# Layer 0 of the second pass by three products of half the columns in place of four

## The reference, cut to what matters

```python
def _layer(x, style, w, b, mw, mb, typ):
    s = style @ mw.T + mb
    weight = SCALE * w * s[:, None, :, None]
    demod = lax.rsqrt(jnp.sum(weight * weight, axis=(2, 3)) + EPS)
    weight = weight * demod[:, :, None, None]
    # 'same': convolution of width 3; 'upsample': transposed one of stride 2, then a blur;
    # 'downsample': blur, then a convolution of stride 2.  Each adds its bias.
...
x = x + _L0_attn_ref(_L0_cond_ref(x, cond, ...), ...)     # four layers, then a long convolution (S4)
x = x + _L0_ffn_ref(_L0_cond2_ref(x, cond, ...), ...)     # four layers, then a routed LoRA layer
# _L0_ffn_ref: xf @ W_base.T + b_base, plus for each row the two best of 8 experts:
#   softmax of their two logits times (xf @ A_e.T) @ B_e.T * 2
```

## Time and profile before

| | |
|---|---|
| median of 3 runs | 1373.13 us (1370.47 to 1373.22) |
| the profiled execution | 1369.01 us, its span 1367.2 us |
| granted TensorE clock, mean | 0.995 |
| PE busy | 1318.5 us (96%), 8319 matmuls |
| DVE busy | 1089.6 us (80%) |
| ACT busy | 821.6 us (60%) |
| POOL busy | 796.6 us (58%) |
| chain that ended last | PE 78%, DVE 11%, ACT 3%, POOL 3% |

### The profile page before, as it was taken

The page is one execution under the profiler, slowest core; times in us unless marked ns, Lnnn a source line. Parts: engine busy times, 40 slices in busy tenths (PEclk is TensorE's granted clock), DMA queues, the critical chain, the costliest instruction groups (busy, mean ns, idle before and its releaser), DMA issues.

```text
span 1367.2 us, 23437 instructions
## 1 busy us (share of the span) xinstructions
PE 1318.5 (96%) x8319; PEld 1245.9 (91%) x8319; DVE 1089.6 (80%) x2613; ACT 821.6 (60%) x1649; POOL 796.6 (58%) x598
## 2 busy tenths in 40 slices
PE   4799999999999999999999999999999999999998
PEld 3588898999899998899999989999999999999998
DVE  7887777777777777778888999788887878788883
ACT  4587777777778787775554444545455554554440
POOL 6367766666667667665555454545555555545542
PEclk9899999999999999999999999999999999999999
DMA  3234444444445564454262432524334252424423
GB/s 130 83 105 130 129 130 130 130 130 129 130 130 137 149 146 122 116 160 113 79 151 76 123 103 76 143 84 121 105 99 128 76 150 76 135 92 116 111 78 90
DMA packets 85990, 158.64 MB, mean 116 GB/s; under 512 B 26473, under 2 KB 47858, under 8 KB 85746
## 3 DMA queue, kind: packets, MB, share of 16 engines
q1 hardware_dynamic: 84610, 155.18, 40.9%
q10 hardware_dynamic: 1264, 1.96, 0.4%
HBM read 94.18 MB, written 33.56 MB: 93 GB/s over the span
## 4 chain that ended last, share of the span: by engine, by line
PE 78%; DVE 11%; ACT 3%; POOL 3%; issue 2%; DMA 2%; SPq 0%; DVEq 0%; POOLq 0%; ACTq 0%
PE psum L1678 25%; PE psum L1680 25%; PE psum L1679 24%; DVE psum L1469 2%; PE psum L1786 1%; DVE vm_l L1437 1%; DMA vm_f<-vv 1%; DMA m0f<-in_m_dram 1%; DVE xr L1486 1%; DVE a_f L1448 1%; DVE a_l L1443 1%; DVE xr L1490 1%; POOL vbuf L848 1%; POOL vbuf L844 1%; ACT u_h L1072 1%
## 5 line engine op out<-in xcount | busy, mean ns | idle before, releaser
L1678 PE MATMUL psum<-wt_h,u_h 128*128 128x386 f32 (+1 forms) x760 | 261.7, 344 | 0.0
L1680 PE MATMUL psum<-wt_h,u_l 128*128 128x386 f32 (+1 forms) x760 | 257.8, 339 | 0.0
L1679 PE MATMUL psum<-wt_l,u_h 128*128 128x386 f32 (+1 forms) x760 | 257.6, 339 | 0.0
L1469 DVE STREAM_TRANSPOSE psum<-vbuf 32x256 f32<-32x256 f32 x480 | 218.8, 456 | 11.8 <-ACT vbuf L1050 0.7
L844 POOL TENSOR_TENSOR vbuf<-vbuf 128x512 f32<-128x512 f32 x64 | 98.7, 1542 | 218.0 <-ACT vbuf L1064 218.0
L1443 DVE SCALAR_TENSOR_TENSOR a_l<-psum,tabs,a_h 128x512 fp32r<-128x512 f32 x128 | 95.7, 751 | 162.9 <-ACT a_h L1032 162.8
L858 POOL TENSOR_TENSOR vm_f<-vm_f 128x512 f32<-128x512 f32 x64 | 82.8, 1293 | 224.3 <-DVE vm_l L1437 224.1
L1678 PE MATMUL psum<-a_h,vm_h 128*128 128x256 f32 x512 | 150.7, 294 | 4.8 <-ACT vbuf L1057 4.7
L1057 ACT ACTIVATE vbuf<-psum,tabs 128x512 f32<-128x512 f32 x128 | 105.6, 825 | 76.4 <-PE psum L1680 74.2
L869 POOL TENSOR_TENSOR xs_l<-xin,xs_h 128x1024 fp32r<-128x1024 f32 x64 | 142.1, 2221 | 14.8 <-ACT xs_h L1018 14.8
L1431 DVE SCALAR_TENSOR_TENSOR vv<-psum,vv 128x192 f32<-128x192 f32 (+2 forms) x384 | 137.2, 357 | 13.2
(11 more groups left out here) (307 smaller groups left out, 3932.6 us busy)
## 6 DMA issues: line engine op xcount, KB each, us to landing
vm_f<-vv SPq DMA_DIRECT2D x256, 112.0 KB, 3.4
xin<-in_x_ph_dram SPq DMA_DIRECT2D x32, 512.0 KB, 4.5
xr<-in_x_row_dram SPq DMA_DIRECT2D x32, 512.0 KB, 5.1
x1d<-xr SPq DMA_DIRECT2D x64, 256.0 KB, 3.3
xin<-x1d SPq DMA_DIRECT2D x32, 512.0 KB, 5.2
xr<-x1d SPq DMA_DIRECT2D x64, 256.0 KB, 5.9
xo<-in_b_base_dram SPq DMA_DIRECT2D x32, 512.0 KB, 4.3
out_dram<-xo SPq DMA_DIRECT2D x31, 512.0 KB, 3.0
```

Of the source, the lines that this page charges most:

```text
L1469: ins = V.transpose(ps_x[to, :, :].rearrange("p b (k n) -> p b k n", n=P)[:, :, :, frm], v3[frm, :, :].rearrange("p b (k n) -> p b k n", n ...
L1678: nc.tensor.matmul(to, stat_h, mov_h, start=first_ and n == 0, stop=False, skip_group_check=True)
L1679: nc.tensor.matmul(to, stat_h, mov_l, start=False, stop=False, skip_group_check=True)
L1680: ins = nc.tensor.matmul(to, stat_l, mov_h, start=False, stop=end, skip_group_check=True)
```

## The change

For tiles from `THREE = TILES + 3` = 35 on, layer 0 is computed from three products over 256 columns of each of the two batches, so each is one bank of 512 columns. With the even and the odd columns of the input apart (`xp`), one product takes the odd columns with the sum of the two matrices (`ms`), and it is shared by the even and the odd output columns; the other two take a difference of neighbouring input columns each (`d0`, and the one that replaces the odd columns in `xin`) with one of the matrices. The shared product goes to `ps_pair`. ACT evacuates it (`odd_product`), DVE adds the two others to it (`halves`), ACT and DVE split the results (`halves_high`, `halves_low`). The column sums are additions on POOL now (`neighbours`), as are the input differences (`differences`). Buffers are reused: `d0` lies in the last part of `vbuf`, its split in the last third of `lag`, the even half and the sums in tables of the first pass.

POOL's new order in `body(i)`: `vs_l`, `combined(i)`, `neighbours(i+1)`, `differences(i+2)`, `column_sums_low(i+1)`, `xo`, `inputs(i+2)`, `pair_sums(i+1)`. ACT: `inputs(i+2)` and `halves_high(i+1)` come before `row_ends(i)`, `pads(i+1)` behind `composed1`. DVE: `halves(i+1)` before the transposes, `halves_low(i+1)` between `router_end` and `composed2`.

```diff
+THREE = TILES + 3
...
+    def three(g):
+        return here(g) and g >= THREE
...
+    d0 = vbuf[:, 2 * H:].rearrange("p (b m) -> p b m", b=2)
+    a_even = old[:, 0:H].rearrange("p (b m) -> p b m", b=2)
+    sums_of = (old[:, H:H + Q], sh.em1[:, 0, :, :].rearrange("p q n -> p (q n)"))
+    msum, ms_h, ms_l = m0f[:, 0, 0, :], m0_h[:, 0, 0, :], m0_l[:, 0, 0, :]
... POOL
+            def differences(g):
+                pool.wait_ge(in_scaled, at(g))
+                pool.wait_ge(v3_val, at(g - 2))
+                G.tensor_scalar(d0[:, :, 0:1], xin[:, :, 0:1], -1.0, None, ALU.mult)
+                G.tensor_tensor(d0[:, :, 1:Q], xin[:, :, 1:H - 1:2], xin[:, :, 2:H:2], ALU.subtract).then_inc(in_diff, 1)
+                pool.wait_ge(in_diff, since(g, 2, 0))
+                G.tensor_tensor(xin[:, :, 1:H:2], xin[:, :, 1:H:2], xin[:, :, 0:H:2], ALU.subtract).then_inc(in_diff, 1)
+            def neighbours(g):
+                pool.wait_ge(y_out, since(g, 2, 1))
+                for b in range(2):
+                    ins = G.tensor_tensor(sums_of[b], a_f[:, b, :], a_even[:, b, :], ALU.add)
+                ins.then_inc(as_sum, 1)
             def inputs(g):
                 pool.wait_ge(in_hi, at(g))
+                if three(g):
+                    G.tensor_tensor(xp_l ..., xin ..., xp_h ..., ALU.subtract)          # 1024 columns, parities apart
+                    G.tensor_tensor(d0_l ..., d0, d0_h ..., ALU.subtract).then_inc(in_lo, 1)   # 512 columns
+                    return
... POOL, body(i)
                 if here(i):
                     combined(i)
+                if three(i + 1):
+                    neighbours(i + 1)
+                if three(i + 2):
+                    differences(i + 2)
+                if three(i + 1):
+                    column_sums_low(i + 1)
...
+                    if three(i + 2):
+                        inputs(i + 2)
                     if here(i + 1):
                         pair_sums(i + 1)
+                    if here(i + 1) and not three(i + 1):
                         column_sums_low(i + 1)
... ACT
+            def odd_product(g):
+                act.wait_ge(as_lo, at(g - 1))
+                act.wait_ge(a_lo, at(g - 1, 2, 1))
+                for b in range(2):
+                    A(a_f[:, b, 0:1], ..., ACT.Identity, bias=...)
+                act.wait_ge(l0_done, at(g, 2, 1))
+                for b in range(2):
+                    ins = A(a_even[:, b, :], ps_pair[:, Q * b:Q * b + Q], ACT.Copy, scale=tab(c, t, b, T_S1))
+                ins.then_inc(shared_out, 1)
+            def halves_high(g):
+                for r, (src, o) in enumerate(((a_f[:, :, :], 1), (a_even, EVEN + 1))):
+                    act.wait_ge(y_out, since(g, 2, r))
+                    A(a_h[:, :, o:o + Q], src, ACT.Copy).then_inc(a_hi, 1)
             def pair_evacuated(g, b):
+                if three(g + 1):
+                    act.wait_ge(in_lo, at(g + 1))
... DVE
+            def halves(g):
+                ve.wait_ge(shared_out, since(g))
+                ve.wait_ge(as_lo, at(g - 1))
+                for r, (to, o) in enumerate(((a_f, 1), (a_even, 0))):
+                    if r:
+                        ve.wait_ge(y_out, since(g, 2, 0))
+                    for b in range(2):
+                        ins = V.scalar_tensor_tensor(out=to[:, b, o:Q], in0=ps_x[:, r, Q * b + o:Q * b + Q],
+                                                     scalar=tabs[:, c, T_S1, batch(t, b)], in1=a_even[:, b, o:Q],
+                                                     op0=ALU.mult, op1=ALU.add)
+                    ins.then_inc(y_out, 1)
+            def halves_low(g):
+                for r, (src, o) in enumerate(((a_f[:, :, :], 1), (a_even, EVEN + 1))):
+                    ve.wait_ge(a_hi, at(g, 2, r))
+                    V.tensor_tensor(a_l[:, :, o:o + Q], src, a_h[:, :, o:o + Q].bitcast(F32), ALU.subtract).then_inc(a_lo, 1)
... DVE, turn(g, 0, 4): waits for v3_fix and y_out of g + 1 in place of v3_fix, a_lo and as_sum
... PE
             def layer0(g):
                 pe.wait_ge(in_lo, at(g))
+                if three(g):
+                    product(ps_x[:, 0, :], [(m0_h[:, c, 0, :], m0_l[:, c, 0, :], d0_h, d0_l)], True, True)
+                    product(ps_x[:, 1, :], [(m0_h[:, c, 1, :], m0_l[:, c, 1, :], xp_h[:, H:L], xp_l[:, H:L])], True, True)\
+                        .then_inc(l0_done, 1)
+                    pe.wait_ge(pair_out, at(g - 1, 2, 1))
+                    product(ps_pair, [(ms_h, ms_l, xp_h[:, 0:H], xp_l[:, 0:H])], True, True).then_inc(l0_done, 1)
+                    return
...
+                    if three(i + 1):
+                        pe.wait_ge(shared_out, since(i + 1))
                     nc.tensor.transpose(ps_hwT, hw[:, :], ident[:, :]).then_inc(pe_hwT, 1)
```

More of the change, by code:

```diff
@@ L905, in body @@
                 else:
+                    if three(i + 2):
+                        inputs(i + 2)
                     if here(i + 1):
                         pair_sums(i + 1)
+                    if here(i + 1) and not three(i + 1):
                         column_sums_low(i + 1)
-                    if here(i + 2):
+                    if here(i + 2) and not three(i + 2):
                         inputs(i + 2)
@@ L1002, in column_sums @@
                 act.wait_ge(as_sum, at(g))
+                if three(g):
+                    for b in range(2):
+                        ins = A(as_h[:, b, 0:Q], sums_of[b], ACT.Copy)
+                    ins.then_inc(as_hi, 1)
+                    return
                 A(as_h[:, :, 0:Q], a_f[:, :, :], ACT.Copy).then_inc(as_hi, 1)
@@ L1138, in body @@
                     A(bt_h, xo[:, :], ACT.Copy, scale=LORA).then_inc(bt_hi, 1)
-                if here(i + 1):
+                if three(i + 1):
+                    odd_product(i + 1)
+                elif here(i + 1):
                     layer0(i + 1)
+                if three(i + 2):
+                    inputs(i + 2)
+                if three(i + 1):
+                    halves_high(i + 1)
                 if by_blocks(i):
@@ L1153, in body @@
                 if here(i + 2):
-                    inputs(i + 2)
+                    if not three(i + 2):
+                        inputs(i + 2)
                     inputs_high(i + 2)
+                if turn_is(i, TILES):
+                    act.wait_ge(ms_sum, 1)
+                    act.wait_ge(l0_done, at(TILES - 1, 2, 1))
+                    A(ms_h, msum, ACT.Copy).then_inc(ms_hi, 1)
                 if chunk(i):
@@ L1162, in body @@
                     composed1(i + 2)
+                if three(i + 1):
+                    pads(i + 1)
                 if turn_is(i, 2):
@@ L1451, in layer0 @@
                 ins.then_inc(as_sum, 1)
+            def halves(g):
+                c, t = place(g)
+                ve.wait_ge(shared_out, since(g))
[3 more added lines that the diff above has]
+                        ve.wait_ge(y_out, since(g, 2, 0))
+                    for b in range(2):
+                        ins = V.scalar_tensor_tensor(out=to[:, b, o:Q], in0=ps_x[:, r, Q * b + o:Q * b + Q],
[6 more added lines that the diff above has]
+                    V.tensor_tensor(a_l[:, :, o:o + Q], src, a_h[:, :, o:o + Q].bitcast(F32), ALU.subtract).then_inc(a_lo, 1)
             def turned(g):
@@ L1464, in turn @@
                     ve.wait_ge(v3_fix, at(g))
-                    ve.wait_ge(a_lo, at(g + 1, 2, 1))
-                    ve.wait_ge(as_sum, at(g + 1))
+                    if three(g + 1):
+                        ve.wait_ge(y_out, since(g + 1, 2, 1))
+                    else:
+                        ve.wait_ge(a_lo, at(g + 1, 2, 1))
+                        ve.wait_ge(as_sum, at(g + 1))
                 for n in range(n0, n1):
@@ L1639, in body @@
                     inserted(i)
-                if here(i + 1):
+                if three(i + 1):
+                    halves(i + 1)
+                elif here(i + 1):
                     layer0(i + 1)
@@ L1653, in body @@
                     router_end(place(i - 1)[1])
+                if three(i + 1):
+                    halves_low(i + 1)
                 if here(i + 1):
```

41 lines of the change are left out of this document (40 added, 1 removed).

## The result

The changed kernel takes 1574.97 us (median of 4 runs, 1573.1 to 1577.73) against 1371.8 (4 runs, 1369.88 to 1373.22): a ratio of 1.1484, 95% interval 1.1459 to 1.1509. Slower, by 203 us, and 2.5 us from the forecast of 1577.5. The profiled execution took 1574.78 us, its span 1572.8.

The account below looks back on a forecast made before the run. PE was taken as the limit by 0.45 us over a 23.29 us loop; 28 turns at 30.95 instead of 23.74 (202) plus edge turns made 204.4 on 1369.0, then 4.1 to the median: 1577.5 us, range 1455 to 1620.

Parts of the forecast that it names:

- Loop and slack: Second pass before the change: the loop over POOL, DVE and ACT takes 23.29 us, 0.45 shorter than PE's turn.
- `halves_low`: DVE between router and `composed2`: two subtractions with both inputs in SBUF add 1.22 us to the loop.
- `xo` against the router: DVE's first router subtraction, wanted at 11.45, waits for POOL's `xo` until 13.5; gates come 1.9 us late, about 15.4.
- GpSimd's inputs: POOL's two instructions, 2.20 and 1.2 us, alternate with DVE's `halves_low` from 15.65, so `vm_l` ends at 21.15.
- The clock: PE idles 4.5 us before the LoRA products, its clock falls, losing 1.7 a turn; 1.2 counts, bounds 0 and 3.0.
- The sum: 28 turns at 30.95 instead of 23.74 give 202 us; the turns before and after add 1.7 and 0.8.
- The faster one: PE stays the limit at the start of `pair(i+1, 1)`, with the loop below 23.04: 1353 us, chance 0.05.
- Only `halves_low`: DVE and POOL get by each other, so each turn loses just 0.77 us: 1395 us, chance 0.07.
- Blocked, clock up: DVE and POOL block each other but PE's clock holds, 6.0 us a turn: 1544 us, chance 0.27.
- Only `xo` blocks: POOL's `inputs` fall between DVE's steps, leaving 2.7 us a turn: 1450 us, chance 0.10.
- signs named in the prediction: Profile after: turns of 29 to 32 us, PE busy 75 to 80%, waiting for `vbuf` too, router and `halves_low` stretched to 1 to 3 us.
- partly blocked case: DVE is held up by POOL's `xo` but not by its `inputs`: 1450 us, chance 0.10.

Follow-up runs that it names:

- second experiment: The changed kernel with GpSimd's `inputs(i+2)` moved behind `pair_sums(i+1)` and `column_sums_low(i+1)` moved behind those inputs: 1428.38 us, ratio 1.0422.
- filler experiment: The changed kernel with 26 unread matmuls of 256 columns put where PE waits for the LoRA operand: 1544.89 us, ratio 1.1272.
- the added pair on DVE: The kernel before with two unread 128x512 subtractions on DVE between `router_end` and `composed2`, tiles 34 to 62: 1396.36 us, ratio 1.0188.

## Why the prediction was right, point by point

**Loop and slack.** 23.29 with 0.45 of slack behind PE was the base of everything. Measured at 23.36 and 23.37.

**`halves_low`.** Priced at 1.22, measured at 1.21 (1006.88 to 1008.09).

**`xo` against the router.** It was to let the first router instruction through at T + 13.5; it ended at T + 13.25 (1005.09). The transpose of the gates was forecast at T + 15.4 and came at 15.18.

**GpSimd's inputs.** Right in sum, wrong in the instruction. The prediction has GpSimd start at T + 15.65, between the two `halves_low`, and alternate with them. In the trace GpSimd starts at T + 15.89, because ACT's split takes 1.99 and not 1.06; both `halves_low` pass at 0.69, overlapped by GpSimd only at the end of the second, and it is the two `vm_l` that are blocked, 4.80 for 1.29. The block in the sum was 2.20 + 1.2 = 3.4 and is 3.51 in the trace: GpSimd's two instructions cost 2.6 and 1.3 undisturbed (2.69 and 1.31 in the second experiment), more than the contiguous 2.20 of the earlier trace rows since they read strided. So `vm_l` ends at T + 21.05 (predicted 21.15), the LoRA operand at 22.03 (22.1), the last transpose at 24.90 (25.0). Late start and longer blocks cancelled against the earlier router; that the end came out within 0.1 is partly luck.

**The clock.** This was the unsure term, taken from one row of before, and it repeats every turn: all 28 turns have a granted clock of 0.89 to 0.95, and 27 of them a wait for `s_h` of 4.42 to 4.45 (one has 3.52). After 4.44 us without a product three matmuls of 256 columns take 0.64 (1016.13 to 1016.77 in the trace of TensorE above), and later in the turn 0.36 (1019.71 to 1020.07). The lower of the two rates, 1.2 GHz, begins in this turn a little behind the wait, at 1014.55, and lasts to 1017.84; then it is 2.4 again. Window and granted clock:

```profile
1014.55:1017.84 3.29, 3.29 (x14) 0.50 0.00 0
991.84:1022.60 30.76, 25.05 (x148) 0.94 0.28 81
```

From the LoRA products to the next T it takes 8.68 where it was 7.07, a loss of 1.61 (predicted 1.7). TensorE's own path, 22.08 + 8.68 = 30.76, closes the turn; the loop would have released it 1.1 earlier (24.90 + 1.82 = 26.72 against 27.87). The prediction took 1.2, and the filler experiment takes 1.0 of it back. What the Trainium skill says in TensorE: Matmul & The Clock Gate, section HAM oscillation — how this bites in real kernels, that waits in each tile bring the half rate back in each tile, the traces here bear out, by these numbers.

**The sum.** 28 turns (642.24 to 1514.90 after, 638.72 to 1310.82 before) are 872.66 against 672.10: 200.6 longer, forecast 202. The remaining 5.0 of the span's 205.6 lie ahead of the first such turn (3.5, of which 1.8 is already there at the start of the second pass) and behind the last (1.5); forecast 2.5. So the terms missed by 1.4 and 2.5 in opposite directions, and the difference of the medians, 203.2 against a forecast of 204.4, is closer than either by luck. The mean turn grew by 7.16, the turn shown by 7.02: two turns near 800 us are longer in both kernels, up to 27.48 before and up to 35.45 after.

**The rivals.** The faster one needed the loop under 23.04. The kernel in which PE has just the nine products, and nothing is added, shows that it isn't: 23.36, and 1359.97 us where the rival's price was 1353. "Only `halves_low`" (1395) is the added pair on DVE, 1396.36: its price was right, and it isn't this kernel. "Blocked, clock up" (1544) is what the filler gives, 1544.89. "Only `xo` blocks" (1450) is the kernel with GpSimd's inputs behind the pair sums, 1460.06: 10 us more, and its handover also waits for `d0`, which the rival did not have. These prices were worked out from rows before any of it ran.

**Signs and chances.** Two of the signs named in the prediction did not come. `halves_low` kept its 0.69 beside the start of GpSimd's work, and the subtractions that stretched are `vm_l`; PE was busy for 82%, not 75 to 80%, and did not wait for `vbuf`, since its own slow products closed the turn. And the range from 1455 on leaves out the partly blocked case at 1450 too, so by the prediction's own chances 0.28 lay outside it, not 0.18.

## What to carry to other kernels

An engine at 100% busy says that it is the limit, not how far the next one is: add up the loop between the engines for one turn before spending work on others to relieve it. Here 20 us of PE time was worth 11 at most. And price an addition on GpSimd by which VectorE instructions it will meet, not by its length: in these traces it was free beside transposes (six in 2.84, with and without) and reads of PSUM (0.87 for two), and beside a VectorE instruction with both inputs in SBUF each held the other up for a whole instruction, be it of one element (1.80 for 0.16). Moving it once more may push it onto something else (another pair of instructions, or the next DMA), so write out both queues for the whole turn.

## What the runs showed of the hardware that I had not expected

- GpSimd's memsets (five of 1024 columns in 5.00 us) leave VectorE's two-input instructions alone and stretch a `TENSOR_SCALAR` of 8 columns from 0.29 to 0.97 and a `CAST` of 8 from 0.16 to 0.33.
- ACT needs 1.99 us to copy 1024 columns with the parities written apart, 1.06 when they are contiguous, and 0.63 to 0.64 for 512 contiguous ones.
- A turn in which TensorE fills the wait with 26 products that nobody reads is 1.0 us shorter (29.74) than one in which it rests for 4.4 us (30.76).
